# Layer 1's expert outputs added to the residual stream by the gathers themselves, instead of gathered to a buffer and added by VectorE

## The reference

```
x = x + xattn0(layernorm(x))     layer 0, windowed cross attention
x = x + ffn0(layernorm(x))       layer 1, 8 experts, the best one per row
x = x + xattn1(layernorm(x))     layer 2, cross attention with 32 keys
x = x + ffn1(layernorm(x))       layer 3, 16 experts, the best three per row, weighted
x = x + xattn2(...); ffn2(...); xattn3(...); ffn3(...)     layers 4 to 7
```

```
gate_logits = x @ gate_w.T + gate_b + expert_bias
top_idx = argmax(gate_logits)
h = relu(x @ w1[e] + b1[e]);  y = h @ w2[e] + b2[e]    for e = top_idx of the row
out = y                                                residual: x = x + out
```

## Time and profile before

| | us |
|---|---|
| median of 3 runs | 740.15 (739.88 to 740.39) |
| the profiled execution | 738.92 |
| its span | 737.1 |
| TensorE busy, of the span | 449.4 (61%) |
| VectorE busy | 389.1 (53%) |
| ScalarE busy | 242.0 (33%) |
| GpSimd busy | 192.3 (26%) |
| layer 1's last store issued | 190.36 |
| layer 1's four additions begin at | 200.16, 208.22, 222.37, 236.39 |

### The profile page before, as it was taken

One profiled execution on the slowest core, in us unless ns is written; L12 is line 12 of the kernel. 1 busy time (PEld: TensorE's weight loads), 2 busy tenths in 40 slices (PEclk: granted clock), 3 DMA queues, 4 the chain that ended last, 5 costly groups with the idle time before them and its releaser, 6 DMA issues.

```text
span 737.1 us, 9512 instructions
## 1 busy us (share of the span) xinstructions
PE 449.4 (61%) x2662; PEld 353.8 (48%) x2662; DVE 389.1 (53%) x1346; ACT 242.0 (33%) x634; POOL 192.3 (26%) x250
## 2 busy tenths in 40 slices
PE   1935964699268862650068888025578998887070
PEld 1834562499236752410067777013455675774050
DVE  2343538465246836720036666044675659965856
ACT  0011101266144640020046666013334465553023
POOL 3010206200352110277700000586631120013002
PEclk9965557699779975675579999556787999997555
DMA  6493001221110700011123333111100000000001
GB/s 178 103 313 124 0 1 36 64 59 45 49 29 23 270 1 0 11 50 53 53 76 101 99 85 85 50 50 35 36 15 1 1 2 0 1 1 1 0 0 57
DMA packets 55884, 39.86 MB, mean 54 GB/s; under 512 B 8900, under 2 KB 50837, under 8 KB 55718
## 3 DMA queue, kind: packets, MB, share of 16 engines
q1 hardware_dynamic: 51750, 31.01, 14.2%
q0 software_dynamic: 4096, 8.40, 3.9%
HBM read 24.18 MB, written 15.20 MB: 53 GB/s over the span
## 4 chain that ended last, share of the span: by engine, by line
PE 35%; DVE 22%; POOL 15%; issue 10%; DVEq 8%; ACT 6%; DMA 3%; SPq 1%; POOLq 0%; ACTq 0%
POOL xbuf L457 8%; PE bank L1605 6%; PE bank L1614 5%; PE bank L1479 4%; POOL wall L465 3%; DVE e_sb L739 2%; ACT xn L1171 2%; POOL rstd L446 2%; DVE mx L735 2%; DVE stats L521 2%; PE bank L1382 2%; PE bank L1469 2%; PE bank L1582 2%; PE bank L1484 1%; PE bank L1510 1%
## 5 line engine op out<-in xcount | busy, mean ns | idle before, releaser
L465 POOL DMA_INDIRECT wall<-ybuf,slots x64 | 61.5, 961 | 172.1 <-DMA ybuf<-h_sb 96.0
L1260 ACT ACTIVATE r<-bank,b1s 128x128 f32<-128x128 f32 x224 | 67.3, 365 | 49.8 <-PE bank L1605 49.8
L457 POOL DMA_INDIRECT xbuf<-h_sb,slots x64 | 63.4, 991 | 70.8 <-DVE slots L890 51.9
L1605 PE MATMUL bank<-on,e_sb 128*128 128x128 f32 x448 | 70.4, 290 | 13.3 <-DVE b1s L927 12.8
L445 POOL TENSOR_SCALAR nmr<-mv 128x4 f32<-128x4 f32 x32 | 7.8, 244 | 237.8 <-DVE veps L528 236.0
L1605 PEld LDWEIGHTS bank<-on,e_sb 128*128 128x128 f32 x448 | 59.2, 198 | 21.6 <-DVE b1s L927 20.5
L917 DVE TENSOR_TENSOR h_sb<-bank,oT 128x128 f32<-128x128 f32 x88 | 25.5, 289 | 81.8 <-PE bank L1614 81.8
L1614 PE MATMUL bank<-eT,r 128*128 128x128 f32 x448 | 66.1, 280 | 0.6 <-issue 0.6
L1614 PEld LDWEIGHTS bank<-eT,r 128*128 128x128 f32 x448 | 57.8, 194 | 1.7 <-issue 1.1
L1469 PE MATMUL bank<-ident,xn 128*128 128x128 f32 x64 | 13.1, 340 | 74.5 <-ACT xn L1171 74.3
L1597 PE MATMUL bank<-ident,h_sb 128*128 128x128 f32 x88 | 24.7, 286 | 54.3 <-DMA h_sb<-xbuf 54.3
(11 more groups left out here) (262 smaller groups left out, 928.3 us busy)
## 6 DMA issues: line engine op xcount, KB each, us to landing
wall<-in_w SPq DMA_DIRECT2D x4, 2048.0 KB, 12.3
h_sb<-xbuf SPq DMA_DIRECT2D x22, 256.0 KB, 2.8
ybuf<-h_sb SPq DMA_DIRECT2D x22, 256.0 KB, 2.3
xbuf<-zero SPq DMA_DIRECT2D x16, 256.0 KB, 3.7
x<-in_x SPq DMA_DIRECT2D x4, 256.0 KB, 3.7
xbuf<-h_sb,slots POOLq DMA_INDIRECT x64, 2.2
wall<-ybuf,slots POOLq DMA_INDIRECT x64, 2.5
b2all<-in_L_ffn_b SPq DMA_DIRECT2D x1, 1024.0 KB, 15.4
```

Source lines behind the costliest of these rows:

```text
L457: nc.gpsimd.indirect_dma_start(xbuf[0:SLOT_TILES[l] * P], bass.IndirectOffsetOnAxis(slots[:, c:c + 1], 0), tile_of(xn_all, t), None).then_ ...
L465: nc.gpsimd.indirect_dma_start(tile_of(yg, t * K + k), None, ybuf[0:SLOT_TILES[l] * P], bass.IndirectOffsetOnAxis(slots[:, c:c + 1], 0)).t ...
L1260: i = a.activation(hT[:, (u % 2) * 512 + c * P:(u % 2) * 512 + (c + 1) * P], bank[2 + u % 2][:, c * P:(c + 1) * P], ACT.Relu, bias=b1s[:, ...
L1605: h = mm(tile_of(bank[2 + u % 2], c), w1s[:, (u % R) * n + c * P:(u % R) * n + (c + 1) * P], tile_of(xsT, u % 2), start=True, stop=True)
```

## The change

In layer 1 an indirect gather gets `compute_op=ALU.add` and the tile of `x` as its destination: the DMA reads the tile, adds the gathered rows and writes it back. `add_experts(1, b)` keeps its wait for `s_gat[b]` and does nothing else. `yg` is used in layer 3 alone. As layer 1 no longer writes to `wall`, the wait for `s_gad` goes, and the semaphore with it. Layer 3's gathers and weighted additions are unchanged.

```diff
@@ SyncE, layer 3's weights
                 else:
-                    sp.wait_ge(s_gad, 4)
                     load(s_wall, wall[:, 0:E * C * P]...)
                     load(s_wall, wall[:, WHALF:WHALF + E * C * P]...)
@@ GpSimd, gather(l, b, part)
-                        nc.gpsimd.indirect_dma_start(tile_of(yg, t * K + k), None, ybuf[0:SLOT_TILES[l] * P], bass.IndirectOffsetOnAxis(slots[:, c:c + 1], 0)).then_inc(s_gat[b], 16)
+                        at = bass.IndirectOffsetOnAxis(slots[:, c:c + 1], 0)
+                        if l == 1:
+                            nc.gpsimd.indirect_dma_start(tile_of(x, t), None, ybuf[0:SLOT_TILES[l] * P], at, compute_op=ALU.add).then_inc(s_gat[b], 16)
+                        else:
+                            nc.gpsimd.indirect_dma_start(tile_of(yg, t * K + k), None, ybuf[0:SLOT_TILES[l] * P], at).then_inc(s_gat[b], 16)
@@ VectorE, add_experts(l, b)
                 dve.wait_ge(s_gat[b], landed[l])
-                if l == 1:
-                    i = v.tensor_tensor(tile_of(x, b, S), tile_of(x, b, S), tile_of(yg, b, S), ALU.add)
-                else:
+                if l == 3:
...
-                i.then_inc(s_gad, 1)
```

More of the change, by code:

```diff
@@ L265, in build @@
         s_gat = [sem(f"s_gat{b}") for b in range(B)]
-        s_gad = sem("s_gad")
         s_h5, s_r5, s_q5 = sem("s_h5"), sem("s_r5"), sem("s_q5")
```

## The result

The changed kernel takes 749.4 us (747.67 to 751.37, 4 runs) where the one before takes 740.27 in the same measurement: 1.0123 of it, 95% interval 1.009 to 1.0157. Measured again later beside the kernel before, it had 1.0141 (1.0102 to 1.0179). The forecast was no change, 740.4 with a range of 736.8 to 744.8. It is outside.

A forecast was written before the change was run, and what follows sets the result against it. A chain changing hands between engines bounds the kernel, with layer 1's gathers and additions a single thread on it. -2.1 (additions) + 0.9 (adding) + 1.5 (early loads) = +0.3 on 740.15 gives 740.4 us, range 736.8 to 744.8.

The forecast's parts named there:

- Part 1: VectorE's additions after layer 1's gathers go: 2.1 us saved, at most 3.1.
- the sum: Additions saved, cost of adding and cost of early loads together: -2.1 + 0.9 + 1.5 = +0.3 us.
- Part 2: Adding gathers cost more to issue on POOL and to land, in batches 0 and 1: 0.9 us, between 0 and 8.7.
- The landing's 0.3: Extra time for an adding gather to land after issue: 0.3 us for each of two landings, batches 0 and 1.
- the first pair of batch 1: First two gathers of batch 1 on POOL: longer issue covered, as POOL idles 1.54 us behind them; cost nothing.
- rival 3: Adding is dear in layer 1's gathers: 4.3 us in place of 0.9, change +3.7, 743.9 us; chance 0.11.
- Part 3: Layer 3's 5 MB of loads move into batch 0's gathers, which they delay: 1.5 us, between 0 and 6.7 for batch 0.
- rival 2: Batch 0's gathers land only when the 5 MB are through: +5.5, 745.7 us; chance 0.12 with lesser such delays.
- Rival 1: Cheap gathers, 738.4 us; if TensorE's clock also holds at batch 2's turns, 1.8 us more, 736.7; chance 0.34.
- the upper ends of parts 2 and 3: Largest costs allowed: 8.7 us for adding gathers, 6.7 us for batch 0's fourth gather served behind the early loads.

The follow-up runs named there:

- m1b: The kernel before, with only batches 2 and 3 adding by DMA and the 5 MB waiting for all of them; ratio 1.0029 (0.9998 to 1.006).
- e1: The changed kernel, but layer 3's 5 MB are issued only when all 16 gathers of layer 1 have landed; ratio 1.0047 against the kernel before.
- e2: The kernel before with plain gathers into another free buffer and no wait, so the 5 MB are issued early; ratio 1.0047.
- e6: The changed kernel with 4 MB in 2 KB rows issued at once and layer 3's 5 MB after the gathers; one run, no ratio, landing 6.8 us.
- e7: The changed kernel with 4 MB in 1 KB rows issued at once and layer 3's 5 MB after the gathers; one run, no ratio, landing 6.6 us.
- e3: Control: the kernel before with layer 1's gathers written to another free buffer, the wait for VectorE's additions kept; ratio 1.0001.
- e4: The changed kernel with only the first 2 MB issued at once, the other loads after all gathers; one run, no ratio, landing 3.4 us.
- m3: The kernel before with batches 2 and 3 adding by DMA, plus 18 extra matmuls and twice two on TensorE; ratio 0.998 (0.9956 to 1.0005).
- a1: The changed kernel itself, measured once more beside the kernel before; ratio 1.0141 (1.0102 to 1.0179).
- w1b: The changed kernel with 22 extra matmuls on TensorE behind layer 1's last, results never read; ratio 1.0136 against the kernel before.
- w4: The kernel before with 18 extra matmuls behind layer 1's last and two each ahead of the turns of batches 1 and 2; ratio 0.9961.

## Why the prediction was wrong

**Part 1 was right as far as the profiles show.** The additions went, and where it can be read the freed place gave what the sum had: 0.72 at batch 2 in m1b (forecast 0.78), nothing at batch 3. No time measured confirms it. At batches 0 and 1 the saving can't be told apart from the delays, but their statistics follow a landing with nothing between.

**Part 2, what adding costs, is the first step that failed: 0.9 us in the sum, 4.3 measured.** The sum took 0.05 us for each issue "as the nearest rows, gather and scatter, differ by 0.3". The trace had 0.6 for each: 1.55 against 0.94. Batch 0 pays three times 0.6 ahead of the fourth gather, batch 1's second pair another 0.6. The landing's 0.3 was 0.8 to 0.9 (3.3 to 3.4 against 2.5), twice. And the first pair of batch 1, put at nothing as POOL idled 1.54 behind it, cost 0.3 in e1. By stages adding costs 0.79 + 1.9 = 2.7 up to batch 0 and 4.3 in all beyond the additions saved (1.9 + 0.9 + two additions of 0.79), against 0.9 in the sum; 8.7 was its upper end. Gather and scatter differ in direction, not in what is asked of the DMA, so neither was near to a gather that adds. The argument against rival 3, that POOL writes "the same list of 128 rows", does not fit the trace: there are 144 packets where there were 32.

**Part 3, what the early loads cost, is the second: 1.5 in the sum, 3.8 with plain gathers, 5.3 with adding ones.** The place was right (batch 0's gathers, loads at 191.6, engines full until 210), and so was that nothing is gained by loading early. The size came from stores that queue behind stores of their own kind. It was taken for the fourth gather's landing alone, but the last store, which the gathers wait for, is also delayed, and the first gather with it by 0.5 us (4.29 against 3.81). The Trainium skill's turns between queues ("DMA: Bandwidth & Descriptors", "Queues, rings and completion order") had given 1.4 by my estimate and 1.8 by its latency under load ("Latency and other measured facts"); e2 measured 3.4 more than without the loads from issue to landing. That the queues take turns agrees with e2, where the gather lands at 206.77 and the loads go on until 211.5, but 3.4 is more than twice the estimate of 1.4, and the estimate took an adding gather for a plain one. An adding one, with 4.5 times the packets, nearly does wait for the end: 208.95 against full engines until 210, and in e6 and e7 it lands within half a us of the fall. That the packets are the cause was not tested by itself. So rival 2, gathers that land when the loads are through, was nearest for the adding gathers, but its landing (206.8), its time (745.7) and its reason were not what came: plain gathers pass the loads.

**The clock was put on one side only.** Rival 1 had it as a possible gain of 1.8 us if an idle time shrank. In the profile after it stays at 0.50 until 234, where before it was back at 1.00 by 212, and filling the gaps puts 2 to 3 us of the loss on it, with an interval that includes zero. As e3 and e4 show, it also differs where the gathers land early, so the late landings are not shown to be its cause. That stays open.

**The sum as measured:** forecast -2.1 + 0.9 + 1.5 = +0.3. At batch 1's statistics the profile has +7.9, of which e1 accounts for 2.7, e2 for 3.8, and the interplay for 1.3. Why the two together cost more than their sum is told by no run. The medians differ by 9.1, so some 1.2 us lie behind that place, where the clock is the candidate. The range too was at fault: the upper ends of parts 2 and 3, 8.7 and 6.7, were on the page, and the range stopped at +4.7 because I took two unknowns to be small together when nothing tied either to its lower end. They came out at half (4.3 of 8.7) and four fifths (5.3 of 6.7) of their upper ends.

## What to carry to other kernels

Letting a gather add saves an engine's addition, but here the transfer itself became longer to issue and to land. It can pay only where the gathers have slack, and even there (m1b, m3) no gain was measured; where a chain waits for them it cost 3.5 us. A wait that guards a buffer may also be what keeps a bulk load away from small transfers on the critical path: before taking it out, look at what will then be in flight together, and put the bulk behind the last small transfer that matters. A price that no row shows keeps its whole range until a run narrows it. And one profile on each side is not enough for a stage whose clock changes between executions: profile a control whose time is unchanged (e3) before a difference there is put down to the change.

## What the runs showed of the hardware

- POOL needs 1.55 us to issue an indirect DMA of 128 rows of 512 bytes that adds into SBUF, 0.94 for the plain one (after, before). With no load beside them the last of a batch lands 3.3 to 3.4 and 2.5 us after its issue began (e1, before). They have 144 and 32 packets.
- Beside 5 MB queued on SyncE's queue a plain gather lands after 5.9 us (e2) and an adding one after 8.2 (after, a1); beside 4 MB an adding one after 6.6 with rows of 1 KB and 6.8 with rows of 2 KB (e7, e6). A store of 256 KB issued just ahead of the loads lands after 2.8 us instead of 2.3 (e2, e1).
- The granted clock of TensorE can be down after long work if a gap follows (3.7 us behind 19 us of matmuls in w1b). In after it was 0.50 from 214 to 234 while TensorE was busy for 15.4 of the 20 us, in e4 from 214 to 232 with 14.2 of 18. Filling TensorE's gaps in that place with matmuls whose results nobody reads was worth 0.39% (0.14 to 0.64) in the kernel before (w4).
